# Keys' projection in two pieces instead of three, and its high part and remainder one score pair sooner

## What is computed

```python
q, k, v = (einsum('oi,bsi->bso', W, layernorm(x)) for W in (Wq, Wk, Wv))      # split into 16 heads of 16
score = where(causal, einsum('bhnd,bhmd->bhnm', q, k) / sqrt(16), -inf)
out = einsum('bhnm,bhmd->bhnd', softmax(score), v)
x = x + layernorm(einsum('oi,bsi->bso', Wo, out))
x = x + layernorm(experts(layernorm(x)))                                       # top 2 of 8, SwiGLU, biases
```

## Time and profile before

| | us |
|---|---|
| median of three runs | 1973.91 (1972.45 to 1975.69) |
| profiled execution | 1974.26 |
| its span | 1972.6 |
| TensorE busy | 1843.6 (93%), weight loads 1325.9 (67%) |
| VectorE busy | 1545.3 (78%) |
| ScalarE busy | 1316.8 (67%) |
| GpSimd busy | 863.7 (44%) |

### The profile page before, as it was taken

How to read it: one execution, slowest core, us unless ns; L and a number is a source line. 1 busy time by engine, 2 the same in 40 slices (tenths; PEclk the granted TensorE clock), 3 DMA queues, 4 the chain that set the end, 5 groups by cost and what they waited for, 6 DMA issues and landing times.

```text
span 1972.6 us, 77603 instructions
## 1 busy us (share of the span) xinstructions
PE 1843.6 (93%) x27790; PEld 1325.9 (67%) x27791; DVE 1545.3 (78%) x5221; ACT 1316.8 (67%) x3291; POOL 863.7 (44%) x1247
## 2 busy tenths in 40 slices
PE   6899999999999999999999899999999999999980
PEld 3255555555555555555554469899999999999970
DVE  3888888888888888888898648778777777777767
ACT  4277788878888888888788765554444545554437
POOL 4323343445546455455454734544333333333336
PEclk9799999999999999999999999999999999999995
DMA  6734656565555646455558569889899999998858
GB/s 199 223 120 128 196 172 206 163 203 180 177 176 165 196 141 199 147 177 181 153 167 246 166 207 271 240 253 259 260 259 264 258 262 263 266 261 245 239 120 341
DMA packets 255070, 411.85 MB, mean 209 GB/s; under 512 B 34480, under 2 KB 191920, under 8 KB 247600
## 3 DMA queue, kind: packets, MB, share of 16 engines
q1 hardware_dynamic: 217856, 363.46, 57.5%
q0 software_dynamic: 27120, 35.40, 10.2%
q10 hardware_dynamic: 9792, 8.93, 1.5%
HBM read 284.83 MB, written 122.28 MB: 206 GB/s over the span
## 4 chain that ended last, share of the span: by engine, by line
PE 82%; DVE 8%; ACT 4%; issue 4%; DMA 2%; SPq 1%; POOL 0%; DVEq 0%; ACTq 0%; POOLq 0%
PE ps_s L1525 18%; PE ps_s L1351 11%; PE ps_w L1351 11%; PE ps_o L1404 10%; PE ps_e L1351 10%; PE ps_e L1525 6%; PE ps_e L1542 6%; PE ps_o L1542 6%; DVE cmax L769 2%; ACT arena L1143 2%; PE ps_e L1535 1%; DVE space L128 1%; DVE arena L766 1%; DVE space L790 1%; PE ps_w L1485 1%
## 5 line engine op out<-in xcount | busy, mean ns | idle before, releaser
L1143 ACT ACTIVATE arena<-ps_e 128x512 f32<-128x512 f32 (+3 forms) x1536 | 688.6, 500 | 190.6 <-PE ps_e L1351 174.9
L766 DVE CUSTOM_DVE_ANT_0 arena<-ps_s,c 128x384 bf16<-128x384 f32 (+3 forms) x1024 | 462.8, 485 | 101.6 <-PE ps_s L1351 93.4
L1351 PE MATMUL ps_s<-arena 96*32 96x512 bf16 (+3 forms) x6144 | 518.1, 333 | 15.0 <-DVE rmax L766 6.8
L1351 PE MATMUL ps_e<-arena 98*32 98x512 bf16 (+3 forms) x6144 | 510.5, 327 | 10.3 <-ACT arena L1143 9.1
L769 DVE TENSOR_REDUCE cmax<-ps_s 128x1 f32<-128x512 f32 x512 | 322.0, 679 | 42.0 <-PE ps_s L1351 41.3
L1404 PE MATMUL ps_o<-arena 128*32 128x256 f32 (+3 forms) x4096 | 344.9, 407 | 2.5 <-POOL arena L663 2.3
L1351 PEld LDWEIGHTS ps_s<-arena 96*32 96x32 bf16 x6144 | 175.9, 96 | 189.7 <-DVE rmax L766 60.6
L1351 PEld LDWEIGHTS ps_e<-arena 98*32 98x32 bf16 x6144 | 179.6, 97 | 149.8 <-issue 36.2
L646 POOL DMA_INDIRECT acc<-blank,place_now x135 | 212.9, 1577 | 147.0 <-DMA acc<-blank,place_now 76.1
L1525 PE MATMUL ps_s<-arena 128*128 128x128 f32 x2192 | 268.7, 276 | 0.0
L663 POOL TENSOR_SCALAR_AFFINE_SELECT arena<-arena 128x512 f32<-128x512 f32 x256 | 162.8, 636 | 239.2 <-ACT arena L1143 238.5
(11 more groups left out here) (182 smaller groups left out, 2720.1 us busy)
## 6 DMA issues: line engine op xcount, KB each, us to landing
arena<-in_gate_up SPq DMA_DIRECT2D x91, 1024.0 KB
arena<-qk_parts SPq DMA_DIRECT2D x384, 128.0 KB
c_h<-in_gate_up SPq DMA_DIRECT2D x44, 1024.0 KB
qk_parts<-space SPq DMA_DIRECT2D x120, 192.0 KB
d_xin<-xs SPq DMA_DIRECT2D x136, 130.5 KB, 3.3
arena<-v_aug SPq DMA_DIRECT2D x32, 512.0 KB, 5.2
o_t<-ot SPq DMA_DIRECT2D x64, 256.0 KB
v_aug<-space SPq DMA_DIRECT2D x28, 512.0 KB, 5.7
```

The source lines that it names most:

```text
L766: dve.tensor_tensor_reduce(summed[:, m % RJ, 0:w], ps_s[:, m % RS, 0:w], after[:, HALF - w:HALF], 1.0, LOWEST, ALU.add, ALU.max, rmax[:, p ...
L1143: act.activation(pw[:, n % RP, 0:w], ps_e[:, n % RE, 0:w], ACT.Exp, scale=SCALE).then_inc(e_done, 1)
L1351: last = pe.matmul(out[at:at + QUAD], lhsT[:, at:at + QUAD], rhs, start=start, stop=stop)
```

## The change

TensorE's keys' projection: steps 0 and 1 together behind pair s=2 of slot 12k-1, steps 2 and 3 together behind pair s=0 of slot 12k. ScalarE's high part of the keys: behind exponential s=1 instead of s=2 of slot 12k. VectorE's remainder of the keys: behind maximum s=2 instead of s=3 of the same slot. Queries, values, second and third parts and all DMAs keep their places.

```diff
@@ vector
                     if s == 2:
+                        for a in due(A_AT, 4, g):
+                            remainder(a, 1)
                         for n in groups_due(25, 22, g):
                             choose(n, 2)
@@ vector, s == 3
                         for a in due(A_AT, 2, g):
                             remainder(a, 0)
-                        for a in due(A_AT, 4, g):
-                            remainder(a, 1)
@@ scalar
+                    if s == 1:
+                        for a in due(A_AT, 4, g):
+                            first_part(a, 1)
                     if s == 2:
...
                         for a in due(A_AT, 3, g):
                             second_part(a, 0)
-                        for a in due(A_AT, 4, g):
-                            first_part(a, 1)
@@ tensor, s == 0
                         for a in due(A_AT, 4, g):
-                            q_or_k(a, 1, (1,))
+                            q_or_k(a, 1, (2, 3))
@@ tensor, s == 1
                         for a in due(A_AT, 2, g):
                             q_or_k(a, 0, (2, 3))
-                        for a in due(A_AT, 4, g):
-                            q_or_k(a, 1, (2, 3))
@@ tensor, s == 2
                         for a in due(A_AT, 3, g):
-                            q_or_k(a, 1, (0,))
+                            q_or_k(a, 1, (0, 1))
```

## The result

The changed kernel takes 1963.13 us (median of 5 runs, 1962.9 to 1965.66) against 1973.91 (5 runs, 1972.45 to 1975.69): ratio 0.9948, 95% interval 0.9934 to 0.9963, so 10.8 us less, and faster by more than the 0.2% that such a measurement can tell. The profiled execution takes 1963.13, its span is 1961.4. The matmul helper L1351 is now L1352 and the transposition L1422 is L1423; L627, L766, L769, L790, L1143 and L1167 keep their numbers.

The account below looks back on a forecast made before the run. TensorE was taken as the bound. 8.6 us from the steady pairs and 3.3 from the four pairs before any score, 11.9 off 1974.26, gave 1962.4, or 1962.0 as median; range for 8 in 10: 1957.5 to 1971.

Parts of the forecast that it names:

- What bounds the kernel: Between 100 and 960 us TensorE is the bound: VectorE waits for it 213 times, 82.8 us; it rarely waits.
- That rival (1970.6): VectorE takes the steady pairs' gain back; only pairs 0 to 3 gain, 3.3 us off; chance 0.10.
- The hole and its three edits, 0.33 per pair: Ahead of the values' projection TensorE loses 0.98 us per period; the edits start the values 0.33 us sooner.
- the step expected to decide: On ScalarE the high part can't precede exponential s=1, pushed back by the joined steps; gain 0.33 of 0.98 us.
- Joining them gains nothing: 0.: TensorE's keys' projection: splitting the four steps costs nothing today, so drawing them together gains 0.
- The steady sum, 26 x 0.33 = 8.6: 26 of 28 later pairs each gain 0.33 us, together 8.6; pairs 4 and 5 count nothing.
- The new wait of TensorE for exponential s=2: Next slot's exponential group goes at about 606.6, not 606.19: 0.4 us wait, costing nothing, with 0.24 us cover.
- The prologue, 3.3: Four pairs projected before any score: holes of 0.84 and 0.83 close, and the DMA chain to first scores moves 3.3 us.
- Each link was seen to wait for the one ahead: Reason given for taking 3.3 us, within bounds 0 to 3.4, for the chain before the first scores.
- What would show it: Hole ahead of the values shrinks from 0.81 to about 0.5, still at line 790; first scores at about 50.
- the third rival: Only pairs 0 to 3 gain, 3.3 us, 1970.6; sign: hole of 0.5 with new TensorE waits for line 766; chance 0.10.
- The whole: Whole kernel: 8.6 plus 3.3, 11.9 us off, 1962.0 us, 0.6% under 1973.91.

Follow-up runs that it names:

- e1: The change made only for pairs 4 to 31, pairs 0 to 3 as in the kernel before: 2017.55 us against 2026.32, ratio 0.9964.
- e4: Kernel before with only ScalarE's high part and VectorE's remainder moved, TensorE's order as before: 2010.88 us, ratio 0.9933.
- e5: Kernel before with high part and remainder moved for all pairs, TensorE's steps joined only for pairs 0 to 3: 1958.35 us, ratio 0.9913.
- e9: Changed kernel with the high part one exponential sooner, behind s=0: 2013.07 us in one execution, against 2025.32 for the kernel before.
- e3: Kernel before with only TensorE's steps moved, for all pairs; high part and remainder stay: 2026.02 us, ratio 1.0004.
- e0_change: Copy of the changed kernel, nothing altered, measured again against the kernel before: 1965.29 us, ratio 0.9944.
- e0_before: Copy of the kernel before, nothing altered, traced again: 1979.95 us in one execution, against 1974.79 for the kernel before in 7 runs.
- e2: The change made only for pairs 0 to 3, later pairs as in the kernel before: 2025.6 us, ratio 1.0005.
- e6: Kernel before with only ScalarE's high part moved, for all pairs: 2021.41 us in one execution, against 2025.32.
- e7: Kernel before with only VectorE's remainder moved, for all pairs: 2026.77 us in one execution, against 2025.32.
- e8: Changed kernel with eight float32 identity multiplications added in TensorE's hole ahead of the first scores: 1963.59 us, ratio 0.9939 against the kernel before.
- e5b: Same kernel as e5, run on the other chip against the kernel before: 2006.93 us against 2025.32, ratio 0.9906.

## Why the prediction was right, point by point

- **What bounds the kernel.** Right. TensorE was the bound: most of what was closed there went to the end (e1 8.8 us where 8.6 were closed, e4 15.4 of 17.9, 26 times 0.69), and e4 and e5 doubled the step per pair by the same reading. The rule of the Trainium skill's page "Perfetto Trace Analysis", section "Identifying the Most-Contended Engine", would have had VectorE (257 of 300 us against 168 of weight loads) take the gain back; e1, with the steady part alone, is 8.8 us faster, so the trace's waits decide against it. That rival (1970.6) did not happen.
- **The hole and its three edits, 0.33 per pair.** Right to 0.02 us in each start that it named in this period, and in the step expected to decide: the high part behind a pushed-back exponential. e4 and e9 show that cause, by taking away what pushed it back (0.69) and by passing it (0.55).
- **"Joining them gains nothing: 0."** Right as it was worded, but half the truth. e3 shows 0.05 lost per pair, so nothing gained; that the joined steps *cost* 0.36 per pair once the other two edits are there follows from the prediction's own next sentence (pair s=1 0.87 later), and it was not put as a price of this edit. A part-by-part sum should have priced the change without this part.
- **The steady sum, 26 x 0.33 = 8.6.** Pairs 7 to 31 gave 8.51: 25 steps, 8.25, less 1.05, plus 1.31 of a stop that e0_change shows to be none of the edits' doing. Pair 6, counted at 0.33, stepped 0.64, and pair 5, counted at nothing, 0.59: the same edits seen from the stretch with maxima alone. The term is right within about 1 us, and part of this is chance.
- **The new wait of TensorE for exponential s=2.** Its place (606.6) was right and that it costs nothing too. The cover of 0.24 us was thin and held.
- **The prologue, 3.3.** This term was mis-sized. TensorE's and GpSimd's part of it came as worked out: holes of 0.84 and 0.83 gone, the step at 32.01 now at 29.79 (forecast 30.05), the last third part 3.58 sooner, 0.31 of which is only that this execution's first remainder came sooner. The premise that the DMA chain behind it would shift as a block failed: the last store took 3.89 against 2.50 us, so 2.4 were left at the first scores, 2.1 without the 0.31. Then the clock fell and 1.0 more went, so that 1.40 is what the prologue has at pair 5's queries, where 3.3 was forecast. That the difference at pair 6's keys is 3.3 again is luck: 1.23 are the own steps of pairs 5 and 6, and 0.67 come in between, where TensorE runs at 0.50 in a later stretch as well, before the change until beyond 90 us (mean of 90 to 94: 0.59), after it until before 90 (mean of 86 to 90: 0.61, then 1.00). e0_before, without the change, gains 0.65 against the kernel before in the same place. e2 says the same by the time: nothing measurable. "Each link was seen to wait for the one ahead" shows that a link binds, not that its duration stays.
- **What would show it.** The line of evidence named for TensorE was wrong: the wait was expected at 0.5 and still put down to line 790, but it is shown as a wait for L1143 of 0.18 and, for the rest, not shown, since modelled matmul ends lie over it. Starts told the truth, idle figures did not. The sign for the third rival, new waits of TensorE for line 766, is absent: 2.2 us in 4 waits, before and after.
- **The whole.** 11.9 forecast, 10.8 measured, by medians, and 9.5 when both kernels were measured once more (e0_change). The steady part carries 8 to 9 of it (e1: 8.8), the prologue the small and unsure rest.

## What to carry to other kernels

When a result is asked for sooner, look at what stands ahead of each of its consumers in that engine's own queue, and at whether the same edit pushes that back: here drawing the producer's steps together delayed the exponential ahead of the consumer, and leaving them apart doubled the gain per pair. Two engines that stand one behind the other in a chain have to be moved together (0.22 and 0 alone, 0.69 both), and a part that is worth nothing by itself should still be tried without. A gain ahead of a chain of DMAs should be counted only as far as the transfers keep their durations, which they did not here.

## What the runs showed of the hardware

**The wait ahead of the first scores can halve TensorE's clock behind it.** The idle time ahead of them and what the first score groups did: full clock throughout behind 1.98 (before), 1.68 (e4), 1.26 (e5), 1.60 (e6), 1.44 (e7) and 0.16 us (e8); a stretch at the lower clock behind 1.98 (e2), 2.19 (e0_change), 2.42 (after), 2.65 (e9), 2.90 (e3), 3.22 (e5b), 3.27 (e0_before) and 3.37 us (e1). 1.98 stands on both sides. Where it falls, it falls between 1.4 us ahead of the first scores' start (e3) and 0.9 us behind it (e0_before). It goes with the wait for the transfer and not with the order of the steps: e0_before and e1 have the old prologue and the fall, e5 the new one and none; and in e8 the wait is taken away and the fall with it. The Trainium skill describes it on the page "TensorE: Matmul & The Clock Gate", section "HAM oscillation — how this bites in real kernels": a wait for a DMA between groups of matmuls makes the next group start at the slow clock. The runs agree in kind.

**A transfer's duration is not a constant of its shape.** The last head load ahead of the first scores takes 2.46 to 2.95 us in most kernels and 4.35 to 4.57 in e0_before, e1 and e5b, in old and new order alike; the last store 2.50 to 2.52 in before, e0_before, e1, e4, e6 and e7, whose prologue has TensorE's old order, and in e3, which has the new one; it takes 3.89 to 3.94 in after, e0_change, e2, e8 and e9, but 2.52 in e5 and 3.47 in e5b, whose prologue is that of the change as well. What sets it was not tried.

**TensorE stops for 1.2 to 2.3 us shortly behind a transfer of instructions.** Six of the 14 traces have such a stop, each between 430 and 438 us and put down to "issue": 2.26 us in e0_before, 1.99 in before, 1.93 in e0_change, 1.71 in e2, 1.18 in e7 and 1.17 in e4. In all six TensorE goes on 2.55 to 2.66 us after the start of a 16 KB transfer on the instruction queue, and the one ahead of that transfer lies 10.7 to 11.7 us back. In the other eight traces two such transfers are at most 10.5 us apart there. The row of the kernel before, for 433.6 to 434.6 us (packets, MB, share):

```profile
q8 instruction: 1, 0.02, 5.7%
```

Shorter stops, 0.3 to 1.1 us, stand between 227 and 234 us in nine traces, 2.4 to 3.0 us behind the start of such a transfer. So TensorE seems to wait for its next instructions; that is read from the times alone, and no run tried it. Two executions of the same program (after, e0_change) differ in it, and it is enough to shift a difference by a tenth of the effect studied.

**One chip is 2.6% slower than the others** (2026 against 1974 us for the kernel before), at a granted clock as high (0.98). Up to 430 us the kernels run there as elsewhere; from there on TensorE falls back by 2.5 to 2.9 us in three quads of four and by about 0.5 in the fourth (e2), with more and longer waits for VectorE (e3: for line 1097, 8.9 us in 14 waits, against 1.1 in 4 for the same line in the kernel before, there 1093). Its cause is open, and so is that of the steps of 0.11 to 0.19 us that the change gives back.
